# Router-weighted tokens made from one transposed copy and coefficients spread over the partitions

## The reference, cut to what matters

```
def _moe_linear(x, router_w, expert_w):      # E = 8, K = 2
    logits = x @ router_w.T
    vals, idx = top_k(logits, K)
    probs = softmax(vals)
    combine = einsum('tk,tke->te', probs, one_hot(idx))
    for e in range(n_exp):
        out = out + combine[:, e:e+1] * (x @ expert_w[e].T)
g = _moe_linear(x, router_gate, w_gate); u = _moe_linear(x, router_up, w_up)
d = _moe_linear(silu(g) * u, router_down, w_down)
x = x + cross(layernorm(x), ctx)    # each block adds to x; x here is 512 tokens x 256
```

## Time and profile before

| | us |
|---|---|
| median of 3 runs | 998.45 |
| lowest, highest | 997.91, 998.53 |
| the profiled execution | 1000.47 |
| its span, first to last instruction | 998.3 |

### The profile page before, as it was taken

The page is one execution under the profiler, slowest core; times in us unless marked ns, Lnnn a source line. Parts: engine busy times, 40 slices in busy tenths (PEclk is TensorE's granted clock), DMA queues, the critical chain, the costliest instruction groups (busy, mean ns, idle before and its releaser), DMA issues.

```text
span 998.3 us, 35149 instructions
## 1 busy us (share of the span) xinstructions
PE 924.5 (93%) x15316; PEld 608.3 (61%) x15316; DVE 606.7 (61%) x1038; ACT 534.7 (54%) x1024; POOL 203.0 (20%) x233
## 2 busy tenths in 40 slices
PE   4679889999899999999999998998899999999998
PEld 2256556656566665666565665666688544446887
DVE  6556665667576466657655866776764774435422
ACT  5367766677666767656575665656635422112100
POOL 4311112121111212111121221313546110000000
PEclk9899999999999999999999999999999999999999
DMA  8677485554634452454344344324221332332100
GB/s 302 207 229 227 116 263 127 159 175 101 187 93 149 136 126 69 126 125 132 96 118 133 90 132 134 77 61 154 87 85 43 133 122 84 104 108 85 43 1 22
DMA packets 70844, 123.83 MB, mean 124 GB/s; under 512 B 34771, under 2 KB 46083, under 8 KB 67429
## 3 DMA queue, kind: packets, MB, share of 16 engines
q1 hardware_dynamic: 69812, 119.84, 40.9%
q0 software_dynamic: 592, 1.42, 0.4%
q10 hardware_dynamic: 288, 0.33, 0.1%
HBM read 64.88 MB, written 17.32 MB: 82 GB/s over the span
## 4 chain that ended last, share of the span: by engine, by line
PE 74%; ACT 9%; DVE 7%; issue 4%; SPq 2%; POOL 2%; DMA 1%; ACTq 0%; POOLq 0%; DVEq 0%
PE ps L716 72%; ACT p L1091 4%; DVE mpart L1331 3%; SPq L471 2%; POOL xg L657 1%; DVE cl L1310 1%; ACT k L1074 1%; ACT kh L1075 1%; DMA c32b<-in_ctxT 1%; ACT ch L1058 1%; PE ps L836 1%; PE ps L866 1%; DVE wl L1362 0%; ACT L1091 0%; ACT wh L1106 0%
## 5 line engine op out<-in xcount | busy, mean ns | idle before, releaser
L1331 DVE TENSOR_REDUCE mpart<-ps 128x2 f32<-128x800 f32 (+1 forms) x256 | 252.4, 988 | 146.6 <-PE ps L716 145.7
L1091 ACT ACTIVATE p<-ps 128x512 f32<-128x512 f32 (+1 forms) x416 | 225.7, 596 | 181.5 <-PE ps L716 180.0
L645 POOL TENSOR_TENSOR kl<-k,kh 128x400 f16<-128x400 f32 (+1 forms) x128 | 120.1, 939 | 446.6 <-ACT kh L1075 446.6
L716 PE MATMUL ps<-p,v 128*17 128x64 f32 x6656 | 130.9, 221 | 0.7 <-ACT p L1091 0.7
L716 PEld LDWEIGHTS ps<-p,v 128*17 128x17 f32 x6656 | 97.5, 98 | 38.1 <-issue 36.9
L716 PE MATMUL ps<-wvh,ch 128*128 128x256 f16 (+1 forms) x416 | 114.6, 275 | 2.2 <-issue 2.2
L716 PE MATMUL ps<-wvl,ch 128*128 128x256 f16 (+1 forms) x416 | 113.4, 273 | 0.0
L716 PE MATMUL ps<-wvh,cl 128*128 128x256 f16 (+1 forms) x416 | 113.4, 273 | 0.0
L716 PE MATMUL ps<-xcl,wh 128*128 128x512 f16 (+2 forms) x384 | 112.8, 308 | 0.0
L716 PE MATMUL ps<-xch,wh 128*128 128x512 f16 (+2 forms) x384 | 112.7, 308 | 0.0
L716 PE MATMUL ps<-xch,wl 128*128 128x512 f16 (+2 forms) x384 | 112.7, 308 | 0.0
(11 more groups left out here) (206 smaller groups left out, 1389.3 us busy)
## 6 DMA issues: line engine op xcount, KB each, us to landing
ks<-kh SPq DMA_DIRECT2D x256, 100.1 KB
w<-in_wgu SPq DMA_DIRECT2D x16, 1024.0 KB, 5.0
ks<-kl SPq DMA_DIRECT2D x128, 100.1 KB
w<-in_wd SPq DMA_DIRECT2D x8, 1024.0 KB, 4.8
c32a<-in_ctxT SPq DMA_DIRECT2D x16, 400.5 KB, 5.0
cparts<-ch SPq DMA_DIRECT2D x8, 800.5 KB, 6.8
cparts<-cl SPq DMA_DIRECT2D x8, 800.5 KB, 8.3
c32a<-in_ctxT SPq DMA_DIRECT2D x12, 400.0 KB, 3.4
```

What stands on the lines that cost most here:

```text
L645: nc.gpsimd.tensor_tensor(kl[:, mt, k0:k0 + w], k32[:, ku % 2, 0:w], kh[:, mt, k0:k0 + w], ALU.subtract).then_inc(sem("klo_done"), 1)
L716: return nc.tensor.matmul(o, lhsT, rhs, start=start, stop=stop, skip_group_check=shared)
L1091: nc.scalar.activation(p32[0:n, step % PRING, BANK * side:BANK * side + BANK], ps[0:n, side, :], ACT.Exp, scale=DH ** -0.5).then_inc(sem(" ...
L1331: nc.vector.reduce_max(mpart[:, j0:j0 + 3:2, quarter], o.rearrange("p (b c) -> p b c", b=2)[:, :, 0:w], AX.X).then_inc(sem("max_done"), 1)
```

## The change

It has five edits.

1. `MID_START` goes from 6 to 3: all events of both layers come three steps earlier, those of the third tile in the last round too.
2. "m_norm" writes `xn` as the other norms do; "m_turn" transposes it once on PE, and ACT copies the result into `xmT` (hidden index on the partitions, 512 tokens along the row), from which "r_logits" reads.
3. The coefficients `cmb` of a tile (128 tokens x 2 maps x 8 experts, tokens on the partitions) are stored to DRAM by SP after "r_pick", and loaded back with every partition receiving all tokens' coefficients: `coef01` (gate, tiles 0 and 1, 1 MB in all partitions), `coef2`, `coef3` (gate, tiles 2 and 3, 0.5 MB each), `coef_up` (up: tiles 0 to 2 in 1.5 MB, tile 3 in 0.5 MB).
4. Scaling an item is now one two-input multiply of `xmT` with a coefficient row that steps over the 8 experts (every eighth f32), repeated for both halves of the width: 128x512 or 128x256, on GpSimd, and on DVE for odd items from 25 on. It is issued at the item's own place, not two items ahead. PE's transposes per item are gone; ACT and DVE read `xg` in SBUF, not PSUM.
5. Items 0 to 7 ride on steps 3 to 10 of the last round; weight blocks 0 and 1 are split in steps 6 and 9 (before: 8 and 11); `TAIL` is reordered, with "u" for ACT's copy. SP's queue takes weight loads 3 to 7 around the coefficient transfers.

```
-MID_START = 6
+MID_START = 3
-SPLIT_AT = {(G - 1, 8): 0, (G - 1, 11): 1}
+SPLIT_AT = {(G - 1, 6): 0, (G - 1, 9): 1}
+X = [(0, e, 0, 2) for e in range(E)] + [(0, e, 2, 3) for e in range(E)] + [(1, e, 0, 2) for e in range(E)] + \
+    [(0, e, 3, 4) for e in range(E)] + [(1, e, 2, 4) for e in range(E)]
+X_AT = {(G - 1, k): k - 3 for k in range(3, 11)}
+TAIL = ("x8 x9 u8 u9 g g out x10 y8 u10 g g g y9 x11 s_norm h2 g s_turn g s_u u11 g s_0 y10 x12 g s_1 y11 x13 u12 "
+        "g s_2 y12 u13 x14 g s_3 y13 u14 x15 g s_4 y14 u15 x16 g s_5 y15 x17 u16 g s_y l2 g g g g_stats y16 u17 "
+        "g g_norm g g y17 x18 g_parts g g u18 x19 y18 g_clean h3 g g g m_stats u19 g m_norm g m_turn l3 g g r_logits "
+        "y19 x20 g g r_pick x21 u20 y20 x22 u21 y21 x23 u22 y22 u23 y23 x24 x25").split()
+for i in range(X_THIRD, X_THIRD + E):
+    TAIL += [f"u{i}", f"y{i}", f"x{i + 2}"]
+held = len(GATE_PARTS) - TAIL.count("g") - E
+TAIL += ["g"] * held
 for n in range(len(LAST_GATE_PARTS)):
+    TAIL += ["d", "g"] if n < E else ["d"]
+TAIL += "u32 y32 x34 h4 l4 u33 y33 x35 u34 y34 x36 u35 y35 h5 l5 x37 u36 y36 x38 u37 y37 x39 u38 y38 u39 y39".split()
...
+        def scaled_by_dve(i):
+            return i > X_THIRD and i % 2 == 1
+        def scaled(eng, i):
+            r, e, t0, t1 = X[i]
+            w = P * (t1 - t0)
+            return eng.tensor_tensor(xg[:, i % 2, :, 0:w], xmT[:, :, P * t0:P * t1],
+                                     coefficients(r, t0, t1)[:, :, e:e + 1].rearrange("p t o -> p o t")
+                                     .broadcast_to([P, KC, w]), ALU.mult)
+            def store_coefficients(t):
+                sp.wait_ge(sem("cmb_done"), t + 1)
+                load(d["coef"][:, P * t:P * t + P, :].rearrange("r p e -> p r e"), cmb[:, t:2 * TT:TT, :], "coef_out")
+            def load_coefficients(dst, r, t0, t1, name):
+                sp.wait_ge(sem("coef_out"), 16 * t1)
+                load(dst.rearrange("p t e -> p (t e)"),
+                     d["coef"][r:r + 1, P * t0:P * t1, :].rearrange("o t e -> o (t e)")
+                     .broadcast_to([P, P * (t1 - t0) * E]), name)
+                elif name == "r_pick":
+                    store_coefficients(t)
+                    if t == 2:
+                        load_coefficients(coef2[:, :, :], 0, 2, 3, "coef2_in")
+                    if (g, k) == (G - 1, 0):
+                        load_coefficients(coef01[:, :, :], 0, 0, 2, "coef01_in")
+                    if (g, k) in ((G - 1, 8), (G - 1, 11)):
+                        load_weight(3 + k // 11)
+            sp.wait_ge(sem("pv_mm"), KT * G)
+            load_coefficients(coef_up[:, 0:3 * P, :], 1, 0, 3, "coef_up_in")
+            load_weight(5)
+            load_weight(6)
+            store_coefficients(3)
+            load_coefficients(coef3[:, :, :], 0, 3, 4, "coef3_in")
+            load_coefficients(coef_up[:, 3 * P:T, :], 1, 3, 4, "coef_up3_in")
...
             def scale_tokens(i):
-                pool.wait_ge(sem("cmb_done"), t1)
-                need(pool, "xcT_mm", i - 1)
-                for t in range(t0, t1):
-                    ins = nc.gpsimd.tensor_scalar(xg[:, i % 2, t - t0, :], xm[:, t, :], cmb[:, TT * r + t, e:e + 1], None,
-                                                  ALU.mult)
-                ins.then_inc(sem(f"xg_ready{i % 2}"), 1)
+                pool.wait_ge(sem(coefficients_in(r, t0, t1)), 16)
+                pool.wait_ge(sem("xnT_ready"), turn_index("m_turn", 1, t1 - 1) + 1)
+                need(pool, "xcl_ready", i - 1)
+                scaled(nc.gpsimd, i).then_inc(sem(f"xg_ready{i % 2}"), 1)
-            def transpose_tokens(i):
...
             def split_tokens(i):
-                act.wait_ge(sem("xcT_mm"), i + 1)
+                act.wait_ge(sem(f"xg_ready{i % 2}"), i // 2 + 1)
+                nc.scalar.activation(xch[r][:, e, :, P * t0:P * t1], xg[:, i % 2, :, 0:P * (t1 - t0)], ACT.Copy)\
+                   .then_inc(sem("xch_ready"), 1)
```

More of the change, by code:

```diff
@@ L112 @@
 LAST_GATE_PARTS = [(n, e, 3, 4) for n in range(GATES) for e in range(E)]
-TAIL = ("x5 g g x6 y5 g y6 g x7 g y7 h2 out x8 h3 g g g g g y8 s_norm s_turn l2 g s_u x9 g s_0 y9 x10 g s_1 y10 x11 g "
-        "s_2 y11 x12 g s_3 y12 x13 g s_4 y13 x14 g s_5 y14 x15 s_y y15 x16 g g g g g_stats y16 x17 g g g g g_norm "
-        "g g g g g_parts g_clean m_stats y17 g g g g g m_norm m_turn l3 g r_logits g g g g g g g g g g g r_pick").split()
-for e in range(E):
-    TAIL += ["g"] * min(2, len(GATE_PARTS) - TAIL.count("g")) + [f"x{X_THIRD + e}", f"y{X_THIRD + e}"]
-TAIL += ["g"] * (len(GATE_PARTS) - TAIL.count("g"))
-TOKENS_AT = dict(zip((1, 3, 5, 7, 9, 15, 17, 19, 21, 23, 25, 27, 29, 30), range(X_BOTH, len(X))))
-for n in range(len(LAST_GATE_PARTS)):
-    TAIL.append("d")
-    if n in TOKENS_AT:
-        TAIL += [f"x{TOKENS_AT[n]}", f"y{TOKENS_AT[n]}"]
-    if n == 9:
-        TAIL += [f"h{GATES}", f"l{GATES}"]
-for w in range(GATES + 1, 2 * GATES):
+TAIL = ("x8 x9 u8 u9 g g out x10 y8 u10 g g g y9 x11 s_norm h2 g s_turn g s_u u11 g s_0 y10 x12 g s_1 y11 x13 u12 "
[6 more added lines that the diff above has]
+TAIL += ["g"] * held
+for n in range(len(LAST_GATE_PARTS)):
+    TAIL += ["d", "g"] if n < E else ["d"]
+TAIL += "u32 y32 x34 h4 l4 u33 y33 x35 u34 y34 x36 u35 y35 h5 l5 x37 u36 y36 x38 u37 y37 x39 u38 y38 u39 y39".split()
+for w in range(GATES + 2, 2 * GATES):
     TAIL += [f"h{w}", f"l{w}"]
@@ L396, in build @@
             wl = sb(s, "wl", [P, W_RING, KC * E * P], F16)
+        with ExitStack() as s:
+            sb(s, "below", [P, 4 * E * KC * T // 4 + W_RING * KC * E * P // 4])
+            coef01 = sb(s, "coef01", [P, 2 * P, E])
         ks.append(sb(ctx, "ks1", [P, NP, S], F16))
@@ L409, in build @@
             ldT = sb(s, "ldT", [E, T])
+        with ExitStack() as s:
+            coef_up = sb(s, "coef_up", [P, T, E])
+            coef3 = sb(s, "coef3", [P, P, E])
         c32 = [c32a[:, 0, :], c32a[:, 1, :], c32b[:, 0, :], c32b[:, 1, :]]
@@ L434, in weight, with coefficients, coefficients_in @@
             return d["wgu"][2 * UNITS[w][1] + UNITS[w][0]] if w < 2 * IT else d["wd"][w - 2 * IT]
-        def token_bank(i):
-            return 6 + i % 2 if i < X_SECOND else i % 2
-        def scaled_by_act(i):
-            return X_BOTH <= i < len(X) and i % 2 == 1
+        def coefficients(r, t0, t1):
+            if r:
+                return coef_up[:, P * t0:P * t1, :]
+            return (coef01[:, :, :], coef01[:, :, :], coef2[:, :, :], coef3[:, :, :])[t0]
+        def coefficients_in(r, t0, t1):
+            if r:
+                return "coef_up_in" if t1 < TT else "coef_up3_in"
+            return ("coef01_in", "coef01_in", "coef2_in", "coef3_in")[t0]
+        def scaled_by_dve(i):
[6 more added lines that the diff above has]
+                                     .broadcast_to([P, KC, w]), ALU.mult)
         def gate_bank(it):
@@ L622, in _ @@
                             load(w32[:, w, :], weight(w), f"w_in{w}")
-            for w in range(3, 2 * IT + E):
-                sp.wait_ge(sem("wlo_done"), w - 2)
-                load(w32[:, w % 3, :], weight(w), f"w_in{w % 3}")
+            sp.wait_ge(sem("pv_mm"), KT * G)
[5 more added lines that the diff above has]
+            load_coefficients(coef_up[:, 3 * P:T, :], 1, 3, 4, "coef_up3_in")
+            for w in range(7, 2 * IT + E):
+                load_weight(w)
             for t in range(TT):
@@ L705, in _ @@
                     event("x", 1, int(item[1:]))
-                else:
+                elif item[0] not in "uy":
                     event(item, 1, TT - 1)
@@ L980, in _ @@
                         last.then_inc(sem("gu_mm"), 1)
-                elif item[0] == "x":
-                    event("x", 1, int(item[1:]))
-                else:
+                elif item[0] not in "xuy":
                     event(item, 1, TT - 1)
             def router_down(it):
+                if it == 0:
+                    pe.wait_ge(sem("exp_done"), 2 * KT * G)
                 pe.wait_ge(sem("inter"), it + 1)
@@ L1235, in _ @@
             for item in TAIL:
-                if item[0] in "xh":
-                    event("x" if item[0] == "x" else "w", 1, int(item[1:]))
-                else:
+                if item[0] in "uh":
+                    event("x" if item[0] == "u" else "w", 1, int(item[1:]))
+                elif item[0] not in "xy":
                     event(item, 1, TT - 1)
```

87 lines of the change are left out of this document (38 added, 49 removed).

## The result

The changed kernel takes 1005.83 us (median of 4 runs, 1004.19 to 1007.54) against 998.49 (997.91 to 999.04) for the kernel before in the same comparison: a ratio of 1.0069, 95% interval 1.0048 to 1.0090. 990.9 was forecast, with a range to 997. The profiled execution took 1005.84, its span is 1004.0, which is 5.7 more than before.

What follows compares the result with a forecast made beforehand. PE was taken to bound the tail, ACT's exponentials the end of the last round. Tail -9.7 (56.4 against 66.1) and last round +2.1 gave -7.6, so 998.45 became 990.9 us, range 984.5 to 997.

Steps and rivals of the forecast that it cites:

- The chain of the fourth tile, 26.2: Tail, "out" to end of r_logits: latency, not PE's work, sets its length; 26.2 us against 25.4 before.
- The sum: Fourth tile's chain: 25.4 - 1.5 + 2.3 = 26.2, with 0.6 for scalings of items 17 and 19 ahead of an inverse root.
- +0.5: Fourth tile's chain: ACT's copy of item 16 comes ahead of the gelu, adding 0.5 us.
- +1.2: Fourth tile's chain: DVE's low half of weight block 2, moved between s_y and g_stats, adds 1.2 us.
- six times 0.25: Fourth tile's scan: six steps each lose a pair of transposes, 1.5 us less in all.
- The last round: Before the first gate part: waits for scaling and router outweigh earlier work; +2.1 us, first gate part at 713.9.
- costed at nothing: Rounds 2 to 14: events three steps earlier cost nothing; with other uncosted edits, within +-1 us in sum.
- Removed transposes: Tail: 108 of the 128 removed transposes lie there and take 11.9 us of PE work with them.
- r_logits to unit 4: End of the tail: 27.6 us of PE work and 1.3 of exposed wait for items, 28.9 in all.
- A scaling on GpSimd: GpSimd's multiply of 128x512 with stepped f32 coefficients: taken as 1.7 us, between 1.16 and 3.03.
- D: Rival, slower: GpSimd's multiply becomes the pace, from 2.4 us per scaling on; 1005 at 3.03 each; chance 0.14.
- A: Rival: PE stays packed, with a shorter chain and scaling near 1.16; 983 to 987; chance 0.17.

Runs made afterwards that it cites:

- e6: The changed kernel with items 16 to 19 scaled by GpSimd in one column instead of all; ratio 0.9996 to the kernel before.
- e7: The changed kernel with twelve held gate parts moved ahead of m_turn; ratio 1.0036 to the kernel before.
- e2: The changed kernel with MID_START back at 6, all else kept; ratio 1.0155 to the kernel before.
- e3: The changed kernel with products of unused results put where PE would wait; ratio 1.0023 to the kernel before.
- e5: The changed kernel with items 0 and 1 scaled earlier, then two items ahead, and weight blocks 0 and 1 split in steps 9 and 11; ratio 1.0003.
- e4: The changed kernel with coefficients read densely, without a step, so tokens get wrong ones; ratio 1.0004 to the kernel before.
- e13: The changed kernel with GpSimd scaling one column of items 2 to 19 except 8 and 16; ratio 0.9966 to the kernel before.
- e14: As e13, with ACT's copy and DVE's low half of those items also one column; ratio 0.9938 to the kernel before.
- e1: The kernel before with MID_START = 3 as its only edit; ratio 0.9975 to the kernel before.
- e10: e8 with products of unused results (6, 6, 64) in the tail where PE would wait; 994.83 us, ratio 0.9929.
- e8: The changed kernel with e5's edits and coefficients transposed by DVE before the store, so reads are dense; ratio 0.9958 to the kernel before.

## Why the prediction was wrong

**The step that failed is "The chain of the fourth tile, 26.2".** It takes 37.6, and 11.4 of the 12.9 us by which unit 4 is late (783.16 against 770.3) are there. Cut at s_y, with the mean clock in the scan (s_0 to s_y); the last column runs to the product behind r_logits, up to 0.15 more than above:

| kernel | "out" to s_y | clock in the scan | s_y to r_logits |
|---|---|---|---|
| before | 14.9 | 1.00 | 10.5 |
| forecast | 13.4 | 1.00 | 12.8 |
| the change | 18.6 | 0.75 | 19.0 |
| e6, items 16 to 19 not scaled | 18.6 | 0.76 | 14.6 |
| e7, parts early | 18.6 | 0.75 | 19.7 |
| e2, late events | 16.8 | 1.00 | 19.4 |
| e3, filler | 15.7 | 1.00 | 19.4 |
| e5, look-ahead | 15.7 | 1.00 | 19.4 |
| e4, dense | 17.1 | 0.91 | 17.6 |
| e13, no scaling | 15.1 | 1.00 | 15.5 |
| e14, bare chain | 14.9 | 1.00 | 13.9 |

- **Behind s_y, GpSimd's scalings: 3.6 (e13, item 16 left whole) to 4.4 (e6).** The sum had 0.6 for them: the inverse roots behind a scaling. What they do besides is to block DVE. I had read the lock in one direction, a low half that lengthens a scaling, and applied it to instructions of DVE with two SBUF inputs. Here three with one input tensor grow by 1.2 to 1.3 each, and `xcl` from 0.69 to 1.27. The Trainium skill (SBUF — State Buffer, Who interferes with whom) says that `tensor_scalar` too may use both of DVE's port pairs and then contends with GpSimd, and that the one that issues first blocks the other; the rows at 740.55, 744.03 and 749.34 agree, and I had left that half of the rule out.
- **Ahead of s_y, mostly the clock.** e13 gains 3.6 here as well, but e3 and e5 gain 2.9 with every scaling in place. What all three share is a scan at clock 1.00; this is read from the traces, as no run changes the clock alone.
- 1.8 are the copies and low halves of the items on ACT and DVE (e14), 1.6 of it behind s_y. The sum had nothing for them: its +0.5 is the copy of item 16 and its +1.2 the low half of weight block 2, and both are still there in e14.
- 2.4 are left (28.6 against 26.2): 1.5 ahead of s_y, 1.0 behind it. I took six times 0.25 off the scan. A step did fall from 1.37 to 1.12, but the last two, 1.01 and 0.63 before, now have a full gate part behind them, and the scan went only from 7.1 to 6.5; the way to its first step went from 7.8 to 8.4. What makes the part behind s_y longer is not taken apart.

**The clock, which I took as 1.00 throughout.** The parts above contain it. A scan step takes 2.00 at half clock in the changed kernel, and 1.12 in e14:

```profile
726.30 0.68 PE L768 MATMUL ps<-st_s,am 64*64 64x126 f32 x2
728.30 0.67 PE L768 MATMUL ps<-st_s,am 64*64 64x124 f32 x2
```

```profile
721.19 0.43 PE L772 MATMUL ps<-st_s,am 64*64 64x126 f32 x2
722.31 0.42 PE L772 MATMUL ps<-st_s,am 64*64 64x124 f32 x2
```

PE's busy time in the tail is 55.9 us in the change (1.56 + 24.60 + 29.70) and 51.7 in e13, for the same products: 4.2 us of slower PE. It is 51.8 in e5 as well, whose waits in the tail are as long as the change's. So a wait can be charged twice, but how long PE waited does not tell by itself whether it is: behind the long wait the products start 0.106 apart in the change, in e5 and in e14, after 10.67, 11.06 and 5.54 us, while the waits of 1.02 and 1.21 are followed by half the clock in the change and not in e5. Why is open.

**The last round: right waits, and two errors that cancel by luck.** First gate part 714.05 (713.9 forecast). ACT idle 3.96 behind the second scaling and 3.50 behind the router (about 3 each forecast). But step 3 to the gate part is 29.7, not 26.1. The router's low half is blocked to 3.37, and without scalings the stretch is 1.2 shorter (e13); PE works here at clock 0.71, and what that costs is not separated. And step 3 starts 3.5 earlier than I had it, most of which goes back to **edit 1, costed at nothing** within 1: the last round starts 3.8 earlier than before (676.1 for 679.9), 2.8 earlier with edit 1 alone on the old kernel (e1, 677.1) and 2.2 later than in the change without it (e2, 678.2). It is worth 2.5 us in the old kernel and 8.6 thousandths in the new one.

**Removed transposes and r_logits to unit 4: right.** PE's work in the tail falls from 62.6 to 51.7 (e13 and e14, where little of it runs at half clock), 10.9 less, with 11.9 counted as removed. 29.6 against 28.9 forecast; the coefficients are in time: the DMA issues of the changed kernel show

```profile
coef_up<-coef SPq DMA_DIRECT2D x1, 1536.0 KB, 9.6
...
coef<-coef SPq DMA_DIRECT2D x2, 512.0 KB, 4.0
...
coef<-cmb SPq DMA_DIRECT2D x4, 8.0 KB, 2.2
```

2.2 for the store (2.6 forecast) and 4.0 for the load (4.4). No wait of PE in the tail is for a transfer or for `xcl`, where I had 1.3; one of 0.3 for `xcl` comes just after unit 4 has begun.

**A scaling on GpSimd: 1.53, I took 1.7.** The size was on the safe side; the Trainium skill's rule (GPSIMD Engine Reference, Performance pitfalls for Q7 kernels) gave 1.74, an estimate, by half as much again. Here the step costs a fifth (1.266 to 1.525), so the direction agrees and the size does not.

**The rivals.** D named the time, 1005, but not the cause: it needed a scaling of over 2.4 and laid 7.9 of its 14.2 on the pairs of items 24 to 39, where PE hardly waits. Its inverse roots behind a scaling are real. A was the furthest off: PE packed needs a chain under 22 us, and it is 28.6 with nearly nothing in the way. What I argued for A, that "today's chain is paced by PE, so its own latency isn't seen", was the point on which the case turned, against A: once PE no longer packs it, the chain takes 28.6 with nearly nothing in its way, more than the 25.4 that it took before. How much of that the new order of the tail adds is not shown. (By the rivals' own parts the chance of faster is 0.78, not 0.80.)

**Still open.** The split of the last round's remaining 2.8 to 4.2 us over e1 (e10 23.8, e8 25.2, e1 21.0), whether the filler in e3 or e10 pays by itself, and what decides the clock in the scan. A dense layout on a kernel with only one of the two queues changed was not tried apart from e4.
